# Splitting whole-array matmuls into column tiles in a four-layer recurrent kernel

## The chip, the cores and the metric

The kernel runs on one core of one Trainium2 chip. The metric is the time of one execution on the device, in microseconds; the time before is a median of three runs. The profile is that of one further execution.

## The reference

x has 32 batch rows, 128 steps and 512 features; every layer adds its result to x. In short form:

```python
x = x + einsum('bsi,io->bso', x * ys[:, None, :], W0) * d[:, None, :]      # L0, scaled by the condition
x = x + rnn(x, h0=cond)            # L1: h = tanh(h @ Wh1 + x_t @ Wx1 + b1), over 128 steps
layer = base[None] + einsum('bdr,bkr->bdk', x_a, x_b)                      # L2, rank 8, one layer per batch row
x = x + (x + einsum('btc,bco->bto', x, layer))
x = x + lstm(x, h0=cond)           # L3: four gates of 512, over 128 steps
```

`x_a` and `x_b` come from a small network on the condition (layernorm, w1, gelu, w2). The low-rank part of L2 is computed as z = x2 · x_a for each batch row, and then z · x_b.

## The kernel before

Data is feature-major: 128 partitions hold a chunk of 128 features, four chunks make 512. The 128 steps are cut into 32 tiles of 4 steps (128 tokens each). Every product in float32 precision is made of three fp16 products, high·high, high·low and low·high, accumulated in PSUM.

The four layers run as a pipeline in one loop over tiles, written out by hand as one order of work for each engine, with semaphores between them. In one turn of the loop TensorE runs, in this order:

- `lstm(t)`, `rnn(r)`, `z(a1)`, `l0(c)`, the first half of `x3_base(a1)`, `rnn(r + 1)`, `lstm(t + 1)`, `gates_x(t + 2)`, `gates_x(t + 3)`,
- `lstm(t + 2)`, `rnn(r + 2)`, the second half of `x3_base(a1)`, `x3_low_rank(a1)`, `l1(c)`, `rnn(r + 3)`, `lstm(t + 3)`, `gates_x(t + 4)`, `gates_x(t + 5)`.

The recurrent products (`rnn`, `lstm`) and `gates_x` have the state or the tokens of one step, 32 columns, as the stationary operand. They are column-tiled: four matmuls, each in its own 32 columns of the array, each with its own weight load (L1525 with 512 or 256 moving columns, L1573 with 128). The dense layers `l0`, `l1`, `x3_base` have a 128x128 block of the weight matrix as the stationary operand and the tile's 128 tokens as the moving one, in whole-array matmuls: 4 output chunks x 12 = 48 for each layer and tile, all through `split_product` (L1461). `z` and `x3_low_rank` go through it too, 24 matmuls of 64 columns each: batch rows are taken in two halves of 16, so that 16 rows x rank 8 fill the 128 partitions. Each matmul is preceded by its weight load.

VectorE masks z (`mask_z`, L1066: of all pairs of a token's and an a's batch row only the equal ones stay), and ScalarE and VectorE then split it into fp16 parts (`zm_high`, `zm_low`). VectorE's order behind `mask_z` in the loop is `zm_low`, `lstm_out`, `x1`, `rnn_sums`, `x1_low`, `rnn_out`, `lstm_gates(t + 1)`; `gates_x(t + 3)` waits for the gate sums (L1096) of the last of these. The start-up computes scales, splits all weights, and makes x_a and x_b in `w2_unit` (L1431) from w2, which streams through a ring of four buffers on SyncE's queue; each load waits for `w2_used`. `turn_a` and `move_b` bring x_a and x_b into their layout; `half_ident` and `same_b` are constants for that and for the mask. The last eight steps of the LSTM (`t >= LATE`) use matmuls of 256 columns.

Of the kernel before, what the change touches and what calls it, by code (L numbers as in the profile page):

```python
# [4 lines left out]
B, T, D, H, RANK = 32, 128, 512, 512, 8  # L5
P = 128
KC = D // P
STEPS = 4
# [6 lines left out]
BH = B // 2  # L15
ZN = STEPS * BH
RING = 4
TOP = 13
# [14 lines left out]
def build(nc, xT, condT, cond, w0, wx1, wh1, b1T, base, hw1, hb1T, hw2, hb2, ln_g, ln_b, wx3, wh3, b3, out):  # L33
# [8 lines left out]
    with ctx:  # L42
        def sb(name, shape, dt=fp32):
            return ctx.enter_context(nc.sbuf_tensor(name, shape, dt))

        def sem(name):
            return ctx.enter_context(nc.semaphore(name))
# [8 lines left out]
        base_hi, base_lo = sb("base_hi", [P, KC, D], fp16), sb("base_lo", [P, KC, D], fp16)  # L56
        a_hi, a_lo = sb("a_hi", [P, 2, KC, P], fp16), sb("a_lo", [P, 2, KC, P], fp16)
        b_hi, b_lo = sb("b_hi", [P, 2, D], fp16), sb("b_lo", [P, 2, D], fp16)
# [27 lines left out]

        half_ident = sb("half_ident", [P, 2, RH * BH])
        same_b = sb("same_b", [P, BH])

# [54 lines left out]
        kept = late[:, 1024:1024 + P]  # L144
        lstm_hs = late[:, 1024 + P:1024 + P + P // 2].bitcast(fp16)
        zm = sb("zm", [P, 2, STEPS, BH])
        zm16 = sb("zm16", [P, 2, 2, STEPS * BH], fp16)
# [61 lines left out]
        consts_ready = sem("consts_ready")  # L209
        folds_ready = sem("folds_ready")  # L210
        ys_ready = sem("ys_ready")
        dve_set = sem("dve_set")
# [53 lines left out]
        xw1_ready = sem("xw1_ready")  # L266
        z_ready = sem("z_ready")
        zm_ready = sem("zm_ready")
        base_ps, lr_ps = sem("base_ps"), sem("lr_ps")
# [22 lines left out]

        def a_turned(n, half):
            return ps_turned[n][:].rearrange("p (c b) -> p c b", b=B)[:, :, BH * half:BH * half + BH]

        def a_part(a, n, half):
            return a[:, half, 2 * n:2 * n + 2].rearrange("p k c -> p (k c)").rearrange("p (c b) -> p c b", b=BH)

# [216 lines left out]
        def _(act):  # L515
# [76 lines left out]
            def a_high():  # L592
                act.wait_ge(a_scale_ready, 1)
                for n in range(2):
                    act.wait_ge(a_ps, n + 1)
                    for half in range(2):
                        high(a_part(a_hi, n, half), a_turned(n, half), s_a).then_inc(a_hi_ready, 1)

# [213 lines left out]
        def _(dve):  # L812
# [174 lines left out]
            def a_low():  # L987
                for n in range(2):
                    dve.wait_ge(a_hi_ready, 2 * n + 2)
                    for half in range(2):  # L990
                        low(a_part(a_lo, n, half), a_turned(n, half), s_a, a_part(a_hi, n, half)).then_inc(a_lo_ready, 1)

# [71 lines left out]
            def mask_z(a):  # L1064
                dve.wait_ge(z_ready, a + 1)
                nc.vector.tensor_tensor(zm[:].rearrange("p h t b -> p (h t) b"),  # L1066
                                        ps_z[:, 0:TOK].rearrange("p (n b) -> p n b", b=BH),
                                        same_b[:].unsqueeze(1).broadcast_to([P, 2 * STEPS, BH]), ALU.mult)\
                  .then_inc(zm_ready, 1)

# [68 lines left out]
            def lstm_out(t):  # L1139
# [3 lines left out]
                if t + 1 < T:  # L1143
# [10 lines left out]
            nc.vector.tensor_reduce(fold[:], ident[:].rearrange("p (k b) -> p b k", b=B), AX.X, ALU.add).then_inc(folds_ready, 1)  # L1154
            nc.vector.tensor_reduce(same_b[:], ident[:].rearrange("p (g b) -> p b g", b=BH), AX.X, ALU.add)\
              .then_inc(folds_ready, 1)
            nc.vector.tensor_copy(half_ident[:].rearrange("p h (j b) -> p h j b", j=RH),
                                  ident[:].rearrange("p (j h b) -> p h j b", j=RH, h=2)).then_inc(folds_ready, 1)

# [238 lines left out]
        def _(pe):  # L1398
# [37 lines left out]
            def turn_a():  # L1436
                pe.wait_ge(rows_ready, 2)
                for n in range(2):
                    for k in range(2):
                        for q in range(2):  # L1440
                            at = P * (2 * k + q)
                            last = nc.tensor.transpose(ps_turned[n][:, at:at + P], a_rows[:, q, P * (2 * n + k):P * (2 * n + k) + P], ident[:])
                    last.then_inc(a_ps, 1)


            def move_b():
                pe.wait_ge(rows_ready, 5)
                pe.wait_ge(l0_scaled, LAG + 1)
                pe.wait_ge(zm_ready, 1)
                for half in range(2):  # L1450
                    for q in range(2):
                        at = BH * RH * q
                        last = nc.tensor.matmul(ps_b[half][at:at + BH * RH, :], half_ident[:, half], b_rows[:, q],
                                                start=True, stop=True, tile_position=(0, at))
                    last.then_inc(b_ps, 1)

            def split_product(psum, w_parts, x_parts):
                (w_hi, w_lo), (x_hi, x_lo) = w_parts, x_parts
                triples = [(w, x) for ws, xs_ in ((w_hi, x_hi), (w_hi, x_lo), (w_lo, x_hi)) for w, x in zip(ws, xs_)]
                for n, (w, x) in enumerate(triples):  # L1460
                    last = nc.tensor.matmul(psum, w, x, start=(n == 0), stop=(n == len(triples) - 1))  # L1461
                return last
# [5 lines left out]
            def dense(psum, w_hi, w_lo, x16, outs):  # L1468
                for oc in outs:
                    last = split_product(psum[:, TOK * oc:TOK * oc + TOK], (chunks(w_hi, oc), chunks(w_lo, oc)),  # L1470
                                         [[x16[:, part, k] for k in range(KC)] for part in range(2)])
                return last

            def of_half(x, half):
# [15 lines left out]
            def z(a):  # L1490
                pe.wait_ge(x2_lo_ready, a + 1)
                wait(pe, zm_ready, a)
                for half in range(2):
                    last = split_product(ps_z[:, ZN * half:ZN * half + ZN],
                                         [[w[:, half, k] for k in range(KC)] for w in (a_hi, a_lo)],
                                         [[of_half(x2_16[:, part, k], half) for k in range(KC)] for part in range(2)])
                last.then_inc(z_ready, 1)
# [80 lines left out]
            pe.wait_ge(consts_ready, 2)  # L1578
            pe.wait_ge(folds_ready, 3)
            pe.wait_ge(ys_ready, 2)  # L1580
# [41 lines left out]
            w2_unit(10)  # L1622
            pe.wait_ge(a_lo_ready, 4)
            z(0)
# [3 lines left out]
            w2_unit(12)  # L1628
            w2_unit(13)
            w2_unit(14)  # L1630
            pe.wait_ge(base_lo_ready, 2)
            x3_base(0, (0, 1))
            w2_unit(15)
            move_b()
            x3_base(0, (2, 3))
# [103 lines left out]
```

## Time and profile before

| | |
|---|---|
| median of three runs | 1146.4 us (1145.34 to 1146.98) |
| time of the profiled execution | 1146.9 us |
| its span, first to last instruction | 1145.1 us |
| mean granted TensorE clock | 0.995 |
| instructions | 56,238 |
| busy: TensorE matmul, weight load | 97%, 66% |
| busy: VectorE, ScalarE, GpSimd | 79%, 37%, 5% |

PE is TensorE's matmuls, PEld its weight loads, which overlap them; DVE is VectorE, ACT ScalarE, POOL GpSimd. Matmuls are pipelined, and the end of one is modelled; so the pace is read from starts. Rows name the tile written, then what is read, then shapes; "x16" counts instructions.

### The profile page before, as it was taken

To read this page: it belongs to the slowest core of one execution; us is meant where nothing else is said; L and a number is where in the kernel's file an instruction comes from. 1 tells how busy PE (TensorE), PEld (TensorE's weight loads), DVE (VectorE), ACT (ScalarE), POOL (GpSimd) and SP (SyncE) were. 2 spreads that over 40 slices of the span, in tenths; PEclk is the share of its full clock that TensorE was granted. 3 is DMA by queue.
4 is the path that set the end of the run, shared out by engine and by line. 5 is a ranking of instruction groups with operands and counts; after the bars stand their busy time and mean duration, and the time that the engine had idled before them with its cause. 6 is when DMAs were issued, how large, how long until landed. Compare 5 with 4: busy or idle time off the path is not lost.

```text
span 1145.1 us, 56238 instructions
## 1 busy us (share of the span) xinstructions
PE 1105.8 (97%) x25596; PEld 752.3 (66%) x25596; DVE 901.8 (79%) x2660; ACT 425.4 (37%) x1036; POOL 54.9 (5%) x75
## 2 busy tenths in 40 slices
PE   5779999999999999999999999999999999999997
PEld 3446666766776676667667666766776676677597
DVE  6897888878878788787778878778878877777665
ACT  6793333333333333333333333333333333333332
POOL 1000000000000000000000000000000000000000
PEclk9989999999999999999999999999999999999999
DMA  9991000000000000000000000000000000000000
GB/s 337 404 364 39 21 21 4 21 21 22 21 22 21 4 21 21 22 22 21 21 12 12 21 22 21 22 21 19 6 21 22 21 21 21 13 3 12 12 14 22
DMA packets 24606, 51.34 MB, mean 45 GB/s; under 512 B 4160, under 2 KB 4288, under 8 KB 23344
## 3 DMA queue, kind: packets, MB, share of 16 engines
q1 hardware_dynamic: 23936, 47.49, 11.7%
q8 instruction: 200, 3.28, 1.2%
q14 instruction: 38, 0.31, 0.1%
q10 hardware_dynamic: 432, 0.26, 0.1%
HBM read 39.36 MB, written 8.39 MB: 42 GB/s over the span
## 4 chain that ended last, share of the span: by engine, by line
PE 91%; DMA 3%; DVE 3%; SPq 1%; ACT 1%; issue 1%; ACTq 0%; DVEq 0%
PE ps_gates L1525 55%; PE ps_l L1461 14%; PE ps_x L1461 7%; PE ps_rnn L1573 7%; DMA ring<-in_hw 3%; PE ps_z L1461 2%; PE ps_lr L1461 2%; PE ps_l L1525 2%; SPq L398 1%; PE ps_gates L1431 1%; DMA rows<-in_ln_b 1%; SPq L429 0%; DVE gates_ring L1096 0%; ACT rows L517 0%; SPq L418 0%
## 5 line engine op out<-in xcount | busy, mean ns | idle before, releaser
L1525 PE MATMUL ps_gates<-big,lstm_h 128*32 128x512 f16 (+1 forms) x6144 | 344.1, 372 | 1.8 <-DVE lstm_h L1129 1.7
L1525 PE MATMUL ps_gates<-big,rows 128*32 128x512 f16 (+1 forms) x6144 | 343.8, 372 | 0.7 <-ACT rows L517 0.6
L1525 PEld LDWEIGHTS ps_gates<-big,rows 128*32 128x32 f16 x6144 | 167.5, 97 | 159.3 <-issue 2.6
L1525 PEld LDWEIGHTS ps_gates<-big,lstm_h 128*32 128x32 f16 x6144 | 160.9, 97 | 146.7 <-DVE lstm_h L1129 2.5
L653 ACT ACTIVATE gates_ring<-gates_ring 128x256 f32<-128x256 f32 x128 | 53.4, 417 | 303.8 <-DVE gates_ring L1096 303.8
L1096 DVE SCALAR_TENSOR_TENSOR gates_ring<-ps_gates,tile_un,rows 128x256 f32<-128x256 f32 x248 | 108.7, 478 | 49.3 <-PE ps_gates L1525 49.2
L1573 PE MATMUL ps_rnn<-wh_hi,rnn_h 128*32 128x128 f16 x4096 | 103.3, 221 | 1.6 <-ACT rnn_h L517 0.7
L1126 DVE SCALAR_TENSOR_TENSOR late<-gates_ring,tile_g,cell_tanh 128x128 f16<-128x128 f32 x127 | 44.6, 352 | 60.2 <-ACT cell_tanh L662 60.2
L1573 PEld LDWEIGHTS ps_rnn<-wh_hi,rnn_h 128*32 128x32 f16 x4096 | 71.9, 97 | 26.5 <-issue 3.8
L1461 PE MATMUL ps_l<-xs,w_hi 128*128 128x128 f16 x1024 | 79.1, 221 | 1.4 <-DVE xs L833 1.4
L1461 PE MATMUL ps_l<-x,wx_hi 128*128 128x128 f16 x1024 | 78.1, 219 | 1.6 <-DVE x L833 1.6
L1461 PE MATMUL ps_x<-x,base_hi 128*128 128x128 f16 x1024 | 78.8, 220 | 0.0
L640 ACT ACTIVATE x_ring<-rnn_pre 128x128 f32<-128x128 f32 x128 | 39.4, 308 | 71.8 <-DVE rnn_pre L924 66.1
L1461 PEld LDWEIGHTS ps_x<-x,base_hi 128*128 128x128 f16 x1024 | 61.5, 98 | 5.0 <-issue 1.8
L924 DVE SCALAR_TENSOR_TENSOR rnn_pre<-rnn_turned,un_rnn,xw1T 128x128 f32<-128x128 f32 x128 | 61.1, 477 | 4.6
L1461 PEld LDWEIGHTS ps_l<-x,wx_hi 128*128 128x128 f16 x1024 | 61.7, 98 | 3.7 <-issue 3.6
L1461 PEld LDWEIGHTS ps_l<-xs,w_hi 128*128 128x128 f16 x1024 | 62.8, 99 | 1.8 <-DVE xs L833 1.7
L517 ACT ACTIVATE rnn_h<-x_ring,scales 128x128 f16<-128x128 f32 x128 | 51.4, 402 | 4.2
L662 ACT ACTIVATE cell_tanh<-cell 128x128 f32<-128x128 f32 x128 | 39.6, 310 | 33.6 <-DVE cell L1116 33.6
L517 ACT ACTIVATE x<-x_ring,tile_s 128x512 f16<-128x512 f32 x32 | 23.1, 722 | 77.7 <-DVE x_ring L935 77.7
L1573 PE MATMUL ps_rnn<-wh_lo,rnn_h 128*32 128x128 f16 x2048 | 51.3, 220 | 0.0
L517 ACT ACTIVATE x<-x1T,tile_s 128x512 f16<-128x512 f32 x32 | 23.1, 721 | 72.6 <-DVE x1T L902 72.6
(199 smaller groups left out, 1614.2 us busy)
## 6 DMA issues: line engine op xcount, KB each, us to landing
ring<-in_hw SPq DMA_DIRECT2D x16, 1024.0 KB, 15.0
xT_sb<-in_xT SPq DMA_DIRECT2D x32, 256.0 KB, 2.8
outT<-late SPq DMA_DIRECT2D x32, 256.0 KB, 2.0
big<-in_wx SPq DMA_DIRECT2D x5, 1024.0 KB, 14.7
big<-in_wh SPq DMA_DIRECT2D x5, 1024.0 KB, 14.3
big<-in_w SPq DMA_DIRECT2D x1, 1024.0 KB, 5.9
big<-in_hw SPq DMA_DIRECT2D x1, 1024.0 KB, 13.6
late<-in_base SPq DMA_DIRECT2D x1, 1024.0 KB, 14.3
```

The costliest lines, as they stand in the source:

```text
L398: sp.dma_start(ring[:, n % RING].rearrange("p (j n) -> p j n", j=RH), hw2[q // 2, RH * (q % 2):RH * (q % 2 + 1), P * k:P * k + P].rearrang ...
L517: return nc.scalar.activation(out_, in_, ACT.Copy, scale=scale)
L640: nc.scalar.activation(x2T[i % X2_RING][:, :, s], rnn_pre[:], ACT.Tanh).then_inc(rnn_h_ready, 1)
L653: nc.scalar.activation(gates[:, 0:2 * P], gates[:, 0:2 * P], ACT.Sigmoid).then_inc(gates_acted, 1)
L662: nc.scalar.activation(cell_tanh[:], cell[:], ACT.Tanh).then_inc(cell_tanh_ready, 1)
L924: nc.vector.scalar_tensor_tensor(rnn_pre[:], rnn_turned[:], un_rnn[:], xw1T[:, :, s], ALU.mult, ALU.add).then_inc(rnn_pre_ready, 1)
L1096: nc.vector.scalar_tensor_tensor(gates[:, columns], psum[:, columns], tile_un[:, a, 0:1], b3_sb[:, columns], ALU.mult, ALU.add).then_inc(g ...
L1126: nc.vector.scalar_tensor_tensor(lstm_hs, gates[:, 2 * P:3 * P], tile_g[:, following, 1:2], cell_tanh[:], ALU.mult, ALU.mult).then_inc(lst ...
L1431: last = nc.tensor.matmul(psum[B * j:B * j + B, columns], hyperT[:, k], ring[:, n % RING, D * j + columns.start:D * j + columns.stop], sta ...
L1461: last = nc.tensor.matmul(psum, w, x, start=(n == 0), stop=(n == len(triples) - 1))
L1525: last = nc.tensor.matmul(by_chunk_of_gate(bank[B * j:B * j + B, columns]), of_step, tile_columns(w, j)[:, gates], start=start, stop=stop, ...
L1573: last = nc.tensor.matmul(by_chunk(ps_rnn[B * j:B * j + B, 0:P]), rnn_h16[:, part, k], hidden_columns(w[:, k], j), start=(n == 0 and k == ...
```

## The change

`split_product` issues each of its products as four matmuls, one for each column tile of 32 output rows; so the dense layers and the low rank have the same number of moving columns, and four times as many matmuls and weight loads. `z` no longer goes through it: x2's tokens become the stationary operand, 32 at a time (a column tile g holds the tokens whose batch row is g modulo 4), and a's columns for those 8 batch rows x 8 ranks, 64 of them, the moving one; 48 matmuls for 24. z then comes out with tokens on the partitions, so `mask_z` transposes it on VectorE in blocks of 32x32 and multiplies each half by the mask. The layout of a, the mask and the constants follow; `move_b` uses whole-array matmuls with four constant matrices (`row_picks`) and is issued in two parts.

```diff
+BG = B // KC
+BQ = BG // 2
...
-        half_ident = sb("half_ident", [P, 2, RH * BH])
-        same_b = sb("same_b", [P, BH])
+        row_picks = sb("row_picks", [P, 2, 2, P])
+        same_b = sb("same_b", [P, BQ, KC])
...
+        def by_rank(x):
+            return x.rearrange("p (k g n q j) -> p k q j n g", k=2, g=KC, n=BG, q=2)
...
                 for n in range(2):
                     act.wait_ge(a_ps, n + 1)
-                    for half in range(2):
-                        high(a_part(a_hi, n, half), a_turned(n, half), s_a).then_inc(a_hi_ready, 1)
+                    high(a_part(a_hi, n), ps_turned[n][:], s_a).then_inc(a_hi_ready, 1)
...
             def mask_z(a):
                 dve.wait_ge(z_ready, a + 1)
-                nc.vector.tensor_tensor(zm[:].rearrange("p h t b -> p (h t) b"),
-                                        ps_z[:, 0:TOK].rearrange("p (n b) -> p n b", b=BH),
-                                        same_b[:].unsqueeze(1).broadcast_to([P, 2 * STEPS, BH]), ALU.mult)\
-                  .then_inc(zm_ready, 1)
+                nc.vector.transpose(z_turned[:], by_chunk(ps_z[:, 0:2 * B])).then_inc(z_turned_ready, 1)
+                dve.wait_ge(z_turned_ready, a + 1)
+                for half in range(2):
+                    own = z_turned[:, half].rearrange("p (t b) -> p t b", t=STEPS)[:, :, BQ * half:BQ * half + BQ]
+                    last = nc.vector.tensor_tensor(zm[:, half].rearrange("p t (b g) -> p t b g", g=KC),
+                                                   own.unsqueeze(3).broadcast_to([P, STEPS, BQ, KC]),
+                                                   same_b[:].unsqueeze(1).broadcast_to([P, STEPS, BQ, KC]), ALU.mult)
+                last.then_inc(zm_ready, 1)
...
-            nc.vector.tensor_copy(half_ident[:].rearrange("p h (j b) -> p h j b", j=RH),
-                                  ident[:].rearrange("p (j h b) -> p h j b", j=RH, h=2)).then_inc(folds_ready, 1)
+            nc.vector.memset(row_picks[:], 0.0).then_inc(picks_cleared, 1)
+            dve.wait_ge(picks_cleared, 1)
+            for q in range(2):
+                for half in range(2):
+                    nc.vector.tensor_copy(row_picks[:, q, half].rearrange("p (g b q j) -> p q g b j", g=KC, b=BQ, q=2)[:, q],
+                                          ident[:].rearrange("p (j h b g) -> p h g b j", j=RH, h=2, b=BQ)[:, half])\
+                      .then_inc(folds_ready, 1)
...
-            def move_b():
-                pe.wait_ge(rows_ready, 5)
-                pe.wait_ge(l0_scaled, LAG + 1)
-                pe.wait_ge(zm_ready, 1)
+            def move_b(q):
+                if q == 0:
+                    pe.wait_ge(rows_ready, 3)
+                    pe.wait_ge(l0_scaled, LAG + 1)
+                    pe.wait_ge(zm_ready, 1)
+                else:
+                    pe.wait_ge(rows_ready, 5)
                 for half in range(2):
-                    for q in range(2):
-                        at = BH * RH * q
-                        last = nc.tensor.matmul(ps_b[half][at:at + BH * RH, :], half_ident[:, half], b_rows[:, q],
-                                                start=True, stop=True, tile_position=(0, at))
-                    last.then_inc(b_ps, 1)
+                    last = nc.tensor.matmul(ps_b[half][:], row_picks[:, q, half], b_rows[:, q], start=(q == 0), stop=(q == 1))
+                    if q == 1:
+                        last.then_inc(b_ps, 1)
...
                 for n, (w, x) in enumerate(triples):
-                    last = nc.tensor.matmul(psum, w, x, start=(n == 0), stop=(n == len(triples) - 1))
+                    for j in range(KC):
+                        last = nc.tensor.matmul(psum[B * j:B * j + B], w[:, B * j:B * j + B], x, start=(n == 0),
+                                                stop=(n == len(triples) - 1), tile_position=(0, B * j))
...
             def z(a):
                 pe.wait_ge(x2_lo_ready, a + 1)
                 wait(pe, zm_ready, a)
-                for half in range(2):
-                    last = split_product(ps_z[:, ZN * half:ZN * half + ZN],
-                                         [[w[:, half, k] for k in range(KC)] for w in (a_hi, a_lo)],
-                                         [[of_half(x2_16[:, part, k], half) for k in range(KC)] for part in range(2)])
+                for n, (part, w) in enumerate(((0, a_hi), (0, a_lo), (1, a_hi))):
+                    for k in range(KC):
+                        for g in range(KC):
+                            last = nc.tensor.matmul(ps_z[B * g:B * g + B, 0:2 * B], of_group(x2_16[:, part, k], g),
+                                                    w[:, k, 2 * B * g:2 * B * g + 2 * B], start=(n == 0 and k == 0),
+                                                    stop=(n == 2 and k == KC - 1), tile_position=(0, B * g))
                 last.then_inc(z_ready, 1)
...
             w2_unit(12)
             w2_unit(13)
+            move_b(0)
             w2_unit(14)
             pe.wait_ge(base_lo_ready, 2)
             x3_base(0, (0, 1))
             w2_unit(15)
-            move_b()
+            move_b(1)
```

## Rows read from the trace of the kernel before

**Rows 1.** The page: busy time and instructions of each engine

```profile
PE 1105.8 (97%) x25596; PEld 752.3 (66%) x25596; DVE 901.8 (79%) x2660; ACT 425.4 (37%) x1036; POOL 54.9 (5%) x75
```

**Rows 2.** The page: DMA queues (packets, MB, share of 16 engines), TensorE instructions

```profile
q8 instruction: 200, 3.28, 1.2%
```

**Rows 3.** Windows (us, busy and count by engine, PEclk, DMA): one tile

```profile
499.80:533.08 33.28, 33.28 (x772) 22.42 (x768) 26.43 (x80) 11.33 (x30) 1.73 (x2) 1.00 0.07 19
```

**Rows 4.** Timeline (start, us, what, count) of TensorE, first run and gates

```profile
503.06 0.40 PE L1573 MATMUL ps_rnn<-wh_hi,rnn_h 128*32 128x128 f16 x16
503.28 0.40 PE L1573 MATMUL ps_rnn<-wh_lo,rnn_h 128*32 128x128 f16 x16
...
503.83 0.41 PE L1461 MATMUL ps_z<-x,a_hi 128*128 128x64 f16 x8
...
504.54 0.61 PE L1461 MATMUL ps_l<-xs,w_hi 128*128 128x128 f16 x8
504.99 0.39 PE L1461 MATMUL ps_l<-xs,w_lo 128*128 128x128 f16 x4
...
509.34 2.76 PE L1525 MATMUL ps_gates<-big,lstm_h 128*32 128x512 f16 x48
511.93 1.25 PE L1525 MATMUL ps_gates<-big,rows 128*32 128x512 f16 x20
```

**Rows 5.** Timeline of TensorE, second run of the same tile

```profile
519.70 0.40 PE L1573 MATMUL ps_rnn<-wh_hi,rnn_h 128*32 128x128 f16 x16
...
521.83 0.22 PE L1461 MATMUL ps_lr<-zm,b_hi 128*128 128x64 f16 x2
...
522.52 0.61 PE L1461 MATMUL ps_l<-x,wx_hi 128*128 128x128 f16 x8
...
525.98 1.25 PE L1525 MATMUL ps_gates<-big,lstm_h 128*32 128x512 f16 x20
```

**Rows 6.** Timeline of VectorE in the same tile

```profile
507.41 0.28 DVE L1066 TENSOR_TENSOR zm<-ps_z,same_b 128x128 f32<-128x128 f32 x1
...
512.97 0.86 DVE L1096 SCALAR_TENSOR_TENSOR gates_ring<-ps_gates,tile_un,rows 128x256 f32<-128x256 f32 x2
```

**Rows 7.** Timeline of the weight loads near the end, idle before in brackets

```profile
1125.00 0.10 PEld L1525 LDWEIGHTS ps_gates<-big,rows 128*32 128x32 f16 x4 [0.42 <-issue]
...
1129.02 0.10 PEld L1525 LDWEIGHTS ps_gates<-big,rows 128*32 128x32 f16 x4 [0.54 <-issue]
...
1132.77 1.29 PEld L1525 LDWEIGHTS ps_l<-big,lstm_h 128*32 128x32 f16 x48 [0.27 <-issue]
...
1136.51 0.10 PEld L1525 LDWEIGHTS ps_gates<-big,rows 128*32 128x32 f16 x4 [0.27 <-issue]
```

**Rows 8.** Windows between such stops

```profile
1097.20:1100.67 3.47, 3.47 (x129) 3.35 (x128) 2.67 (x9) 0.46 (x2) 0.00 (x0) 1.00 0.04 9
1125.00:1129.01 4.01, 3.68 (x128) 3.48 (x128) 2.42 (x9) 0.68 (x3) 0.00 (x0) 1.00 0.02 4
1129.01:1132.75 3.74, 3.68 (x128) 3.48 (x128) 2.37 (x9) 0.62 (x3) 0.00 (x0) 1.00 0.02 4
1132.75:1136.50 3.75, 3.68 (x128) 3.48 (x128) 2.09 (x7) 1.29 (x4) 0.00 (x0) 1.00 0.02 4
```

**Rows 9.** DMA of 1126.0 to 1127.6: forty slices, and the queue

```profile
GB/s 0 0 410 0 0 0 0 0 0 0 0 0 0 0 0 0 0 0 0 0 0 0 0 0 0 0 0 0 0 0 0 0 0 0 0 0 0 0 0 0
...
q8 instruction: 1, 0.02, 5.5%
```

**Rows 10.** Timeline of TensorE in the start-up

```profile
61.30 0.23 PE L1573 MATMUL ps_rnn<-wh_hi,rnn_h 128*32 128x128 f16 x2 [0.46 <-issue]
```

**Rows 11.** Windows in the start-up, PEclk the third number from the end

```profile
79.50:82.90 3.40, 1.49 (x24) 0.41 (x16) 3.40 (x5) 2.67 (x3) 0.00 (x0) 1.00 1.04 380
82.90:86.30 3.40, 3.04 (x28) 1.77 (x29) 2.99 (x3) 2.19 (x2) 0.00 (x0) 0.50 0.33 124
```

**Rows 12.** Waits of TensorE: waiting for what, us in total, times, longest

```profile
PE ps_gates L1431 <- DMA ring<-in_hw: 11.3, 7, 4.1
```

More of the change, by code:

```diff
@@ L56, in build @@
         base_hi, base_lo = sb("base_hi", [P, KC, D], fp16), sb("base_lo", [P, KC, D], fp16)
-        a_hi, a_lo = sb("a_hi", [P, 2, KC, P], fp16), sb("a_lo", [P, 2, KC, P], fp16)
+        a_hi, a_lo = sb("a_hi", [P, KC, 2 * P], fp16), sb("a_lo", [P, KC, 2 * P], fp16)
         b_hi, b_lo = sb("b_hi", [P, 2, D], fp16), sb("b_lo", [P, 2, D], fp16)
@@ L145, in build @@
         lstm_hs = late[:, 1024 + P:1024 + P + P // 2].bitcast(fp16)
+        z_turned = sb("z_turned", [P, 2, B])
         zm = sb("zm", [P, 2, STEPS, BH])
@@ L210, in build @@
         folds_ready = sem("folds_ready")
+        picks_cleared = sem("picks_cleared")
         ys_ready = sem("ys_ready")
@@ L267, in build @@
         z_ready = sem("z_ready")
+        z_turned_ready = sem("z_turned_ready")
         zm_ready = sem("zm_ready")
@@ L291, in build, with a_part @@
         out_ready = sem("out_ready")
[L293 to L297, printed above, removed]
+        def by_rank(x):
+            return x.rearrange("p (k g n q j) -> p k q j n g", k=2, g=KC, n=BG, q=2)
+        def a_part(a, n):
+            return a[:, 2 * n:2 * n + 2].rearrange("p k c -> p (k c)")
         def by_row(w):
@@ L988, in a_low @@
                 for n in range(2):
-                    dve.wait_ge(a_hi_ready, 2 * n + 2)
-                    for half in range(2):
-                        low(a_part(a_lo, n, half), a_turned(n, half), s_a, a_part(a_hi, n, half)).then_inc(a_lo_ready, 1)
+                    dve.wait_ge(a_hi_ready, n + 1)
+                    low(a_part(a_lo, n), ps_turned[n][:], s_a, a_part(a_hi, n)).then_inc(a_lo_ready, 1)
             def base_diagonal():
@@ L1154, in _ @@
             nc.vector.tensor_reduce(fold[:], ident[:].rearrange("p (k b) -> p b k", b=B), AX.X, ALU.add).then_inc(folds_ready, 1)
-            nc.vector.tensor_reduce(same_b[:], ident[:].rearrange("p (g b) -> p b g", b=BH), AX.X, ALU.add)\
+            nc.vector.tensor_reduce(same_b[:], ident[:].rearrange("p (g b r) -> p b g r", g=KC, b=BQ), AX.X, ALU.add)\
               .then_inc(folds_ready, 1)
-            nc.vector.tensor_copy(half_ident[:].rearrange("p h (j b) -> p h j b", j=RH),
-                                  ident[:].rearrange("p (j h b) -> p h j b", j=RH, h=2)).then_inc(folds_ready, 1)
+            nc.vector.memset(row_picks[:], 0.0).then_inc(picks_cleared, 1)
[5 more added lines that the diff above has]
+                      .then_inc(folds_ready, 1)
             dve.wait_ge(ld_cond, 16)
@@ L1440, in turn_a @@
                         for q in range(2):
-                            at = P * (2 * k + q)
-                            last = nc.tensor.transpose(ps_turned[n][:, at:at + P], a_rows[:, q, P * (2 * n + k):P * (2 * n + k) + P], ident[:])
+                            last = nc.tensor.transpose(by_rank(ps_turned[n][:])[:, k, q],
+                                                       a_rows[:, q, P * (2 * n + k):P * (2 * n + k) + P], ident[:])
                     last.then_inc(a_ps, 1)
-            def move_b():
-                pe.wait_ge(rows_ready, 5)
-                pe.wait_ge(l0_scaled, LAG + 1)
-                pe.wait_ge(zm_ready, 1)
-                for half in range(2):
-                    for q in range(2):
-                        at = BH * RH * q
-                        last = nc.tensor.matmul(ps_b[half][at:at + BH * RH, :], half_ident[:, half], b_rows[:, q],
-                                                start=True, stop=True, tile_position=(0, at))
-                    last.then_inc(b_ps, 1)
+            def move_b(q):
[5 more added lines that the diff above has]
+                    pe.wait_ge(rows_ready, 5)
+                for half in range(2):
+                    last = nc.tensor.matmul(ps_b[half][:], row_picks[:, q, half], b_rows[:, q], start=(q == 0), stop=(q == 1))
+                    if q == 1:
+                        last.then_inc(b_ps, 1)
             def split_product(psum, w_parts, x_parts):
@@ L1472, in dense, with of_group @@
                 return last
+            def of_group(x, g):
+                return x.rearrange("p (n g) -> p g n", g=KC)[:, g]
             def of_half(x, half):
@@ L1492, in z @@
                 wait(pe, zm_ready, a)
-                for half in range(2):
-                    last = split_product(ps_z[:, ZN * half:ZN * half + ZN],
-                                         [[w[:, half, k] for k in range(KC)] for w in (a_hi, a_lo)],
-                                         [[of_half(x2_16[:, part, k], half) for k in range(KC)] for part in range(2)])
+                for n, (part, w) in enumerate(((0, a_hi), (0, a_lo), (1, a_hi))):
[4 more added lines that the diff above has]
+                                                    stop=(n == 2 and k == KC - 1), tile_position=(0, B * g))
                 last.then_inc(z_ready, 1)
@@ L1578, in _ @@
             pe.wait_ge(consts_ready, 2)
-            pe.wait_ge(folds_ready, 3)
+            pe.wait_ge(folds_ready, 6)
             pe.wait_ge(ys_ready, 2)
@@ L1622, in _ @@
             w2_unit(10)
-            pe.wait_ge(a_lo_ready, 4)
+            pe.wait_ge(a_lo_ready, 2)
             z(0)
```

## The prediction

> **What bounds the kernel now.** I read the page first, then the windows of one tile, then the order of time on TensorE, and last the issue gaps near the end. The page shows TensorE busy for 97% of the span [rows 1]. In the middle of the loop that is no average over good and bad stages: the window of one tile, 33.28 us, is busy for all of it, at a granted clock of 1.00 [rows 3]. So in the loop every us that TensorE gains or loses is a us of the result, unless something else ends last.
>
> The order of time gives the paces. Column-tile matmuls of 128 columns (rnn) come in fours, one per tile: sixteen take 503.28 - 503.06 = 0.22 us, so a four takes 55 ns [rows 4]. A whole-array matmul of 128 columns takes 0.45/8 = 56 ns. So the split costs no array time by itself. The 48 of rnn would be through at 503.06 + 3 x 0.22 = 503.72, yet the first z matmul starts at 503.83: changing between column tiles and the whole array costs about 0.10 us [rows 4]. A tile changes four times, so 0.41 us go there. z takes 0.71 us (24 matmuls of 64 columns, 29.6 ns each) [rows 4], the low rank 0.69 us for as many [rows 5].
>
> The view that decides is another one. TensorE runs 25,596 matmuls and as many weight loads [rows 1], and the instruction queue brought 200 packets of 16.4 KB [rows 2]: 3.28 MB over 51,192 instructions is 64 bytes each, so one packet is a page of 256 instructions, 128 pairs. Near the end TensorE's weight loads stop again and again "on issue", with no semaphore named: at 1125.00, 1129.02, 1132.77 and 1136.51 [rows 7]. Between one of these stops and the next lie exactly 128 weight loads and 128 matmuls [rows 8]: the stops are page turns. The same kind of gap stands in the start-up, at 61.30 us [rows 10].
>
> What a turn costs: from one starved turn to the next took 4.01, 3.74 and 3.75 us; one more page, from 1097.20 on, took 3.47 us, all of it filled with work [rows 8]. After the turn at 1125.00 the next page's packet starts in the third of forty slices of its window, about 1.1 us later, and moves for 5.5% of 16 x 1.6 us = 1.4 us [rows 9]; the next turn at 1129.02 comes 1.5 us after that. So a page is asked for when the one before it is entered, one at a time, and is there 1.1 + 1.4 + 1.5 = 4.0 us later. Over the run a packet took 1.2% x 16 x 1145.1 / 200 = 1.1 us [rows 2], so 3.7 us is the usual case. **I take 3.7 us per page, with 3.5 and 4.0 as bounds.** In the loop this hides today, barely: the stretch from rnn to rnn around z and l0 holds 384 instructions in 509.34 - 503.06 = 6.28 us [rows 4], 4.2 us per page, and its twin around the low rank as many in 6.28 us [rows 5].
>
> The Trainium skill says otherwise: "Runtime: NRT & Kernel Launch", section "Instruction fetch mechanics", gives TensorE an instruction buffer of 128 KiB (2,048 instructions), refilled in 16 KiB blocks, the crossing mostly hidden. The block size agrees with the trace; the depth does not, since a turn waits for the very next page here. By that rule the fetch would cost nothing (first rival).
>
> **The change part by part, for one tile of the loop.**
>
> Dense layers and low rank: 3 x 48 + 24 = 168 whole-array matmuls become 672; z's 24 become 48. A tile goes from 768 pairs (772 with those in flight at the edges of the window) [rows 3] to 768 + 504 + 24 = 1,296 pairs, 2,592 instructions, 10.1 pages for 6.0.
>
> Array time: z in twelve fours of 64 columns. The trace shows no such four; its cost lies between 29.6 ns (one z matmul) and 55 ns (an rnn four). I take the first, since the fours of 128 columns stream at the pace of one matmul: 12 x 29.6 = 0.36 us, 0.36 less (0.05 at the other bound). The low rank's fours lie between the same bounds: nothing, to +0.62 us. The dense layers: nothing. Four changes of mode gone: -0.41. Together 0.77 us less, **if instructions arrive**.
>
> They do not. The gates' matmuls of 512 columns take 511.93 - 509.34 = 2.59 us per 96 instructions [rows 4], 6.9 us a page, and hide any fetch. Between them lie two runs. Run 1 (rnn, z, l0, half of x3_base, rnn) becomes 96 + 96 + 384 + 192 + 96 = 864 instructions; at the array's own pace 6.28 - 0.20 - 0.36 = 5.72 us, 6.6 ns each, 1.70 us a page. Run 2 (rnn, half of x3_base, low rank, l1, rnn) becomes 96 + 192 + 192 + 384 + 96 = 960; 6.28 - 0.20 = 6.08 us, 1.62 us a page. A run starts and ends somewhere inside a page: on average the first half page was asked for in the gates and is there, the last half runs at its own pace, and the F/256 - 1 pages between cost 3.7 us each.
> - Run 1: 2.375 x 3.7 + 1.70 = 10.5 us for 6.28.
> - Run 2: 2.75 x 3.7 + 1.62 = 11.8 us for 6.28.
> - The page that a run ends in was asked for at its last turn; where more than about 157 of its 256 instructions belong to the run, the gates wait for the next one too: in 4 of 10 cases, 1 us on average, twice: +0.7.
>
> Sum: 4.2 + 5.5 + 0.7 = **+10.4 us per tile, 29 tiles: +302 us**. At 3.5 us a page it is 5.1 x 0.2 = 1.0 less per tile, at 4.0 us 1.5 more: +272 to +345.
>
> mask_z: one VectorE instruction of 0.28 us [rows 6] becomes a transpose and two half-size products behind a wait. No row shows these; each has half the elements, so between 0.14 and 0.28 us, 0.42 to 0.84 together. I take 0.62, +0.34. Behind it on VectorE stand zm_low, x1, rnn_sums and the gate sums, which end at 512.97 + 0.86 = 513.83 [rows 6]; TensorE needs them about 514.3 (half-way through the two gates_x, one four ahead). Today 0.34 us would nearly fill that room; with TensorE 4 us later in run 1 it is covered. If that cover is gone, see the first rival.
>
> Start-up: l0, l1 (three each), one x3_base, one low rank and one z add 7 x 288 + 144 + 48 = 2,208 instructions, 8.6 pages at 2.0 us more than their own pace: +17. TensorE waits 11.3 us there for w2's transfers [rows 12], which cover part. I take +8, with 0 and +25 as bounds. move_b's first half (two whole-array products for two split ones) goes into such a wait, its second half costs what the whole did. row_picks, a_high and a_low are set-up in waits: nothing, at most +1.
>
> End: two more rounds of z, x3_base and low rank add 960 instructions, 3.75 pages, in a stage already at the page's pace, partly under waits for lstm_h: +6 (2 to 12).
>
> Clock: where TensorE was busy 1.49 of 3.40 us, the granted clock of the next 3.4 us was 0.50, the lower level [rows 11]. The new runs are busy 1.7 of 3.7 us, about that. Inside a run the lower clock costs little (32 fours at twice 55 ns are 3.5 us, under 3.7), but gates behind it would run at half pace until the clock is back: at most 1.7 us per run, 3.4 per tile. I take 0.5 per tile, +15; bounds 0 and +99.
>
> Sum against the profiled execution (span 1145.1, its time 1146.9, 0.5 over the median): 1146.9 + 302 + 8 + 6 + 15 = **1478 us**.
>
> **The rivals.**
> 1. *The fetch stays hidden*: TensorE holds several pages ahead, and a turn never waits. Then 0.77 us per tile are free, but run 1's 0.56 meet VectorE: its chain to the gate sums does not shrink and grows by 0.34, against some 0.42 us of room, so that stretch keeps about 0.1; run 2 keeps 0.2. 29 x 0.3 = 9, and 2 at the ends: 1136 us; 1123 if VectorE kept up. It decides from the point where a page turn costs less than 1.7 us. Against it: three pages in a row of 3.7 to 4.0 us, each ended by a gap [rows 7, 8]. 5%. The page of the Trainium skill named above would give this case.
> 2. *A starved sequencer asks earlier*, so that transfer and landing alone count, 1.1 + 1.5 = 2.6 us: runs of 7.9 and 8.8 us, +4.1 per tile, 1146.9 + 119 + 8 = 1274 us. Against it: the packet of [rows 9] started 1.1 us after the turn, though TensorE was starving. 6%.
> 3. *The clock falls behind each run*: 1478 + 29 x 2.9 = 1562 us. For it stands [rows 11]; against it, that runs at the lower clock are busy enough to bring it back. 12%.
> 4. *No change within 0.2%*: a page of about 2.0 us would do it; nothing points there. 1%.
>
> **How the numbers follow.** The forecast has 76%. Its own range is 1440 to 1540 (page 3.5 to 4.0 us, the start-up's bounds). To leave out no more than 2 in 10, I reach up into rival 3 and a little below for pages that overlap with gates better than on average: 1395 to 1580. A measurement of this kernel tells 0.2% from no change; faster 5%, same 1%, slower 94%.
>
> **What the profile afterwards would show.** TensorE's busy share falls to about 80%, with gaps "on issue" inside l0, l1, x3_base and the low rank, 128 pairs apart; the instruction queue brings some 330 packets; a tile takes about 44 us; no gap at the old changes of mode; z fours 29.6 ns apart; VectorE's share falls. I am wrong if 128 pairs of l1 pass in 1.8 us, or if the gaps name a semaphore; too low if the granted clock falls well under 0.9.

## The result, and the profile after

The changed kernel takes 1454.7 us (median of six runs, 1450.64 to 1469.17) for 1145.05 (six runs): a ratio of 1.272, 95% interval 1.266 to 1.278. It is slower by 310 us. 1478 was forecast, with a range of 1395 to 1580. The profiled execution is the slowest of the six, 1469.2 us, so the rows below hold some 14 us more than the median.

The page after, against [rows 1, 2]: TensorE's busy share, the granted clock in forty slices, the instruction queue.

```profile
PE 1165.1 (79%) x42492; PEld 853.1 (58%) x42492; DVE 902.8 (62%) x2726; ACT 426.8 (29%) x1034; POOL 54.4 (4%) x75
...
PEclk9789999999999999989999999989999999999999
...
q8 instruction: 332, 5.44, 1.5%
```

TensorE is busy for 79% (forecast: about 80%), and the queue brought 332 packets (forecast: some 330) for 200. Its busy time grew by 59 us only; 263 us of the 322 by which the span grew are time in which it does nothing. The two spans, cut at the first matmul of `rnn(8)`, in the loop's first turn, and of `rnn(124)`, 29 turns later; windows as in [rows 3], of the changed kernel:

```profile
0.00:125.86 125.86, 82.87 (x2271) 50.48 (x2273) 83.10 (x216) 74.00 (x102) 6.28 (x19) 0.86 0.72 261
125.86:1384.18 1258.32, 1011.49 (x37591) 743.79 (x37587) 769.19 (x2343) 331.05 (x869) 48.10 (x56) 0.97 0.05 16
1384.18:1467.37 83.19, 70.73 (x2645) 58.85 (x2637) 50.53 (x167) 21.78 (x63) 0.00 (x0) 0.98 0.04 14
```

and of the kernel before:

```profile
0.00:102.92 102.92, 71.63 (x1164) 44.26 (x1168) 82.56 (x212) 74.17 (x104) 6.66 (x19) 0.95 0.87 318
102.92:1068.80 965.88, 965.48 (x22276) 649.94 (x22272) 769.47 (x2285) 329.57 (x869) 48.23 (x56) 1.00 0.06 18
1068.80:1145.14 76.34, 68.67 (x2164) 58.08 (x2156) 49.76 (x163) 21.68 (x63) 0.00 (x0) 1.00 0.04 14
```

The start-up took 22.9 us more, the loop 292.4 (10.1 per tile), the end 6.9. What TensorE waited for inside the loop (waits: us, times, longest us):

```profile
PE ps_l L1475 <- issue: 137.7, 85, 2.6
PE ps_x L1475 <- issue: 37.1, 22, 2.1
PE ps_lr L1475 <- issue: 29.5, 20, 1.9
PE ps_rnn L1593 <- issue: 28.4, 19, 2.0
PE ps_gates L1545 <- issue: 13.0, 14, 2.0
```

246 us, and all of it "issue": no semaphore, no engine and no transfer of data is named. The only row beside these is a single wait of 0.7 us for VectorE. The timeline of the second run of one tile (starts and, in brackets, idle time before), to be held against [rows 5]:

```profile
666.96 0.40 PE L1593 MATMUL ps_rnn<-wh_hi,rnn_h 128*32 128x128 f16 x16
...
667.62 0.63 PE L1475 MATMUL ps_x<-x,base_hi 128*32 128x128 f16 x32
...
670.95 0.21 PE L1475 MATMUL ps_lr<-zm,b_hi 128*32 128x64 f16 x4 [1.60 <-issue]
...
672.22 0.35 PE L1475 MATMUL ps_l<-x,wx_hi 128*32 128x128 f16 x11
674.80 0.49 PE L1475 MATMUL ps_l<-x,wx_hi 128*32 128x128 f16 x21 [2.23 <-issue]
...
677.31 0.54 PE L1475 MATMUL ps_l<-x,wx_lo 128*32 128x128 f16 x11
678.54 0.37 PE L1475 MATMUL ps_l<-x,wx_lo 128*32 128x128 f16 x5 [0.69 <-issue]
...
679.41 2.79 PE L1545 MATMUL ps_gates<-big,lstm_h 128*32 128x512 f16 x48
```

The run takes 679.41 - 666.96 = 12.45 us for 6.28. It stops three times, in the middle of the low rank and twice in the middle of l1's products, where nothing is being waited for. The windows between the stops count the instructions:

```profile
670.94:674.79 3.85, 1.63 (x127) 1.46 (x128) 2.24 (x6) 1.41 (x2) 0.00 (x0) 1.00 0.02 4
674.79:678.53 3.74, 3.06 (x128) 2.85 (x128) 0.18 (x1) 0.00 (x0) 0.00 (x0) 0.59 0.02 4
```

The DMA's view of the 2 us behind the first stop shows what is on its way (forty slices, and the queue):

```profile
GB/s 0 0 0 0 0 0 0 0 0 0 0 0 0 0 0 0 0 0 0 0 0 0 328 0 0 0 0 0 0 0 0 0 0 0 0 0 0 0 0 0
...
q8 instruction: 1, 0.02, 4.2%
```

Again 128 weight loads and 128 matmuls, a page, in 3.85 and 3.74 us, of which TensorE worked for 1.63 in the first. The next page's packet starts in the 23rd of forty slices, 671.0 + 22 x 0.05 = 672.1, 1.15 us after the turn at 670.95. It moves for 4.2% of 16 x 2 us = 1.34 us, to 673.5, and the next turn comes 1.3 us later: the three parts of [rows 9] again. These two pages are no exception: in the trace of the loop one such stop follows another with just one page between them 95 times, and from stop to stop it takes 3.74 us on average, 3.45 to 4.12.

In the second window the granted clock is 0.59, after a page in which the array had been busy for 1.63 of 3.85 us. Where it falls late in a run, the gates behind the run pay, as behind the first run of this tile (timeline of TensorE, and the window of the first twelve fours):

```profile
654.85 4.52 PE L1545 MATMUL ps_gates<-big,lstm_h 128*32 128x512 f16 x48
659.18 5.36 PE L1545 MATMUL ps_gates<-big,rows 128*32 128x512 f16 x96
664.37 2.77 PE L1545 MATMUL ps_gates<-big,lstm_h 128*32 128x512 f16 x48
```

```profile
654.85:659.18 4.33, 4.33 (x59) 1.95 (x52) 1.69 (x4) 0.71 (x2) 0.00 (x0) 0.59 0.02 4
```

Twelve fours take 659.18 - 654.85 = 4.3 us there, busy throughout, at a granted clock of 0.59; the twelve that start at 664.37 are through at 666.96, 2.6 us later, as in [rows 4].

### The profile page after: what moved, and what is told of

It reads as the page before. It is cut to its first block, busy times and chain, and to the rows that moved or that the text cites. A ratio compares the mean times of both kernels' runs of the same rounds, so it can differ in the third digit from the quotient of the medians.

```text
span 1467.4 us, 90094 instructions
## 1 busy us (share of the span) xinstructions
PE 1165.1 (79%) x42492; PEld 853.1 (58%) x42492; DVE 902.8 (62%) x2726; ACT 426.8 (29%) x1034; POOL 54.4 (4%) x75
## 4 chain that ended last, share of the span: by engine, by line
PE 78%; issue 19%; DVE 2%; ACT 1%; DMA 1%; ACTq 0%; DVEq 0%
PE ps_gates L1545 45%; PE ps_l L1475 14%; PE ps_rnn L1593 6%; PE ps_x L1475 6%; PE ps_lr L1475 2%; PE ps_l L1545 1%; PE ps_z L1514 1%; PE ps_gates L1443 1%; DMA rows<-in_ln_b 1%; DVE big L837 0%; DVE gates_ring L1103 0%; PE ps_lr L1443 0%; ACT big L522 0%; PE ps_l L1466 0%; PE ps_gates L1438 0%
## 5 line engine op out<-in xcount | busy, mean ns | idle before, releaser
L1545 PE MATMUL ps_gates<-big,lstm_h 128*32 128x512 f16 (+1 forms) x6144 | 366.5, 381 | 14.9 <-issue 13.4
L1475 PE MATMUL ps_l<-x,wx_hi 128*32 128x128 f16 x4096 | 96.4, 230 | 65.2 <-issue 65.2
L1475 PE MATMUL ps_l<-xs,w_hi 128*32 128x128 f16 x4096 | 90.3, 224 | 44.7 <-issue 42.7
L1475 PEld LDWEIGHTS ps_l<-x,wx_hi 128*32 128x32 f16 x4096 | 73.4, 102 | 70.4 <-issue 70.4
L1475 PE MATMUL ps_x<-x,base_hi 128*32 128x128 f16 x4096 | 88.2, 222 | 23.0 <-issue 23.0
L1475 PEld LDWEIGHTS ps_l<-xs,w_hi 128*32 128x32 f16 x4096 | 68.9, 99 | 50.1 <-issue 47.7
L1475 PEld LDWEIGHTS ps_x<-x,base_hi 128*32 128x32 f16 x4096 | 70.5, 98 | 26.0 <-issue 25.9
L1475 PE MATMUL ps_l<-x,wx_lo 128*32 128x128 f16 x2048 | 62.2, 232 | 25.6 <-issue 25.6
L1475 PE MATMUL ps_l<-xs,w_lo 128*32 128x128 f16 x2048 | 58.2, 224 | 20.7 <-issue 20.7
L1475 PE MATMUL ps_x<-x,base_lo 128*32 128x128 f16 x2048 | 59.7, 223 | 16.3 <-issue 16.1
L1475 PEld LDWEIGHTS ps_l<-x,wx_lo 128*32 128x32 f16 x2048 | 43.5, 104 | 30.3 <-issue 30.3
```

Of the source, the lines that this page charges most:

```text
L1475: last = nc.tensor.matmul(psum[B * j:B * j + B], w[:, B * j:B * j + B], x, start=(n == 0), stop=(n == len(triples) - 1), tile_position=(0, ...
L1545: last = nc.tensor.matmul(by_chunk_of_gate(bank[B * j:B * j + B, columns]), of_step, tile_columns(w, j)[:, gates], start=start, stop=stop, ...
```

## The experiments

The times of before on the same chip were 1144.8 us (the first four) and 1145.4 (the others).

**1. Column tiles for z alone.** `split_product` is whole-array again; everything else is as changed.

```diff
-                    for j in range(KC):
-                        last = nc.tensor.matmul(psum[B * j:B * j + B], w[:, B * j:B * j + B], x, start=(n == 0),
-                                                stop=(n == len(triples) - 1), tile_position=(0, B * j))
+                    last = nc.tensor.matmul(psum, w, x, start=(n == 0), stop=(n == len(triples) - 1))
```

> The changed kernel with the dense layers and the low rank whole-array again: only z's column tiles, its mask and layout are new. A tile has 792 pairs for 768. Page theory (a page of 128 pairs takes 3.7 us from being asked for to being there, and only short runs of TensorE that cross pages pay): 1,584 instructions per tile, the runs stay near 3.4 us a page, nothing is starved; TensorE saves up to 0.36 us per tile and VectorE's longer mask takes some of it back: 1141 us, 1134 to 1150. Rival, every added column-tile pair costs the same (the 310 us over 29 tiles and 528 pairs are 20 ns each): 24 pairs, +0.5 us per tile, 1160 us. Rival, the longer mask delays the gates: +0.3 us per tile, 1155 us.

1141.35 us, ratio 0.9969 (0.9956 to 0.9981): 0.3% faster, and where the page theory put it. z's part of the change isn't what costs; all that was lost belongs to the split. z in the timeline of TensorE:

```profile
501.00 0.30 PE L1512 MATMUL ps_z<-a_hi,x 128*32 128x64 f16 x16
...
501.26 0.33 PE L1512 MATMUL ps_z<-a_hi,x 128*32 128x64 f16 x16
501.52 0.62 PE L1474 MATMUL ps_l<-xs,w_hi 128*128 128x128 f16 x8
```

The mask in the timeline of VectorE:

```profile
504.69 0.24 DVE L1069 STREAM_TRANSPOSE z_turned<-ps_z 128x64 f32<-128x64 f32 x1
504.96 0.36 DVE L1073 TENSOR_TENSOR zm<-z_turned,same_b 128x64 f32<-128x64 f32 x2
505.70 0.29 DVE L837 SCALAR_TENSOR_TENSOR zm<-zm 128x128 f16<-128x128 f32 x1 [0.38 <-ACT zm L522]
```

z and the change of mode behind it take 501.52 - 501.00 = 0.52 us; with 0.10 for the change of mode, z's twelve fours take 0.42 (forecast 0.36, bounds 0.36 and 0.66). The mask takes 505.32 - 504.69 = 0.63 us (forecast 0.62). From `rnn(8)` to `rnn(124)` a tile takes 33.15 us for 33.31 before, less than the first run alone gained.

**2. The split alone.** The kernel before, with the change's `split_product`.

```diff
-                    last = nc.tensor.matmul(psum, w, x, start=(n == 0), stop=(n == len(triples) - 1))
+                    for j in range(KC):
+                        last = nc.tensor.matmul(psum[B * j:B * j + B], w[:, B * j:B * j + B], x, start=(n == 0),
+                                                stop=(n == len(triples) - 1), tile_position=(0, B * j))
```

> The kernel before with only the split of the dense layers and the low rank; z stays whole-array. Page theory: 2,544 instructions per tile for 2,592, the two runs have 816 and 960: a tile of 43.2 us at 3.7 us a page, 1446 us, 1425 to 1465. Rival, z's new form and its mask are what costs: about 1146 us. Equal cost of each added pair does not differ here (504 of 528 pairs: 1440 us).

1495.0 us, ratio 1.306, above the stated range: the expectation had counted wrongly. In the kernel before z goes through `split_product` too, so the edit makes 96 column-tile pairs of z's 24, where the expectation left z alone. The page (TensorE, instruction queue):

```profile
PE 1170.1 (78%) x44028; PEld 858.0 (58%) x44028; DVE 891.1 (60%) x2660; ACT 426.9 (29%) x1036; POOL 54.2 (4%) x75
...
q8 instruction: 344, 5.64, 1.6%
```

44,028 matmuls, 1,536 more than the change's 42,492, which is 48 for each of 32 tiles. 96 instructions more in the first run are 96 / 256 x 3.7 = 1.39 us a tile, 40 us over 29 tiles; the kernel takes 1495.0 - 1454.7 = 40.3 us more than the change. The number on record was a miss, and the agreement afterwards is in part luck: between the two traces a tile grows by 0.83 us only (44.22 for 43.39; 24 us over 29 tiles), the first run by 1.07 (11.40 for 10.33) where 1.39 are worked out. That the first run pays for the added instructions is shown, the price of 3.7 us only roughly.

**3. Two column tiles of 64 rows** for four of 32, in all that the change splits.

```diff
-                    for j in range(KC):
-                        last = nc.tensor.matmul(psum[B * j:B * j + B], w[:, B * j:B * j + B], x, start=(n == 0),
-                                                stop=(n == len(triples) - 1), tile_position=(0, B * j))
+                    for j in range(2):
+                        last = nc.tensor.matmul(psum[2 * B * j:2 * B * j + 2 * B], w[:, 2 * B * j:2 * B * j + 2 * B], x, start=(n == 0),
+                                                stop=(n == len(triples) - 1), tile_position=(0, 2 * B * j))
```

> The changed kernel with the split in two column tiles of 64 output rows for four of 32: 960 pairs per tile for 1,296 (768 before). Page theory: the two runs have 576 instructions each, 2.2 pages, of which some 1.2 turns lie inside and about half are hidden by the gates beside them; replayed at 3.7 us a page a tile takes 34.1 us: +0.85 us over 29 tiles and about 8 at the start, 1178 us, 1160 to 1195. Rival, each added pair costs 20 ns: 192 pairs, +3.8 us per tile, 1256 us. Rival, column tiling of these products costs whatever the number of tiles: over 1400 us.

1165.0 us, ratio 1.0175 (1.016 to 1.019). The cost is not so much per pair: 192 of the 528 added pairs per tile, 36%, bring 20 of the 310 us, 7%. A tile takes 33.88 us (forecast 34.1), and the start-up loses nothing (`rnn(8)` at 102.8 us), where 8 was expected. The timeline shows one thing more:

```profile
493.62 0.40 PE L1593 MATMUL ps_rnn<-wh_hi,rnn_h 128*32 128x128 f16 x16
493.95 0.64 PE L1475 MATMUL ps_x<-x,base_hi 128*64 128x128 f16 x16
```

The last sixteen of rnn would be through at 493.62 + 0.22 = 493.84; the first product in tiles of 64 rows starts 0.11 us later. Going from tiles of 32 to tiles of 64 costs what going to the whole array costs [rows 4]. The Trainium skill's "TensorEngine Tiling (Array Packing)", section "Key Properties", says that changing the tiling mode drains the engine; this agrees.

**4. The same tiles in fewer instructions.** The dense layers with tokens as the stationary operand. Those layers' results have tokens where the reference has features.

```diff
-                for oc in outs:
-                    last = split_product(psum[:, TOK * oc:TOK * oc + TOK], (chunks(w_hi, oc), chunks(w_lo, oc)),
-                                         [[x16[:, part, k] for k in range(KC)] for part in range(2)])
+                columns = slice(P * outs[0], P * outs[-1] + P)
+                pairs = [(part, w, k) for part, w in ((0, w_hi), (1, w_hi), (0, w_lo)) for k in range(KC)]
+                for n, (part, w, k) in enumerate(pairs):
+                    for j in range(KC):
+                        last = nc.tensor.matmul(psum[B * j:B * j + B, columns], x16[:, part, k, B * j:B * j + B], w[:, k, columns],
+                                                start=(n == 0), stop=(n == len(pairs) - 1), tile_position=(0, B * j))
```

> The changed kernel with the three dense layers turned round: the tokens are the stationary operand, 32 to a column tile, the weights the moving one, 512 columns (256 in the halves of the base layer). Column tiles, products and array time are those of the change (12 fours of 216 ns for 48 of 56 ns), in a quarter of the instructions (half for the base layer): 912 pairs per tile. The dense layers' results come out with tokens on the partitions, which the rest takes as if they were features. Page theory: runs of 480 and 576 instructions, a tile of 33.4 us at 3.7 us a page, 1150 us, 1135 to 1165. Rival, column tiling of these products is what costs: like the change, 1455 us. Rival, 20 ns for each added pair: 144 pairs, 1230 us.

1157.2 us, ratio 1.0107 (1.009 to 1.012). Against the change, the column tiles and the number of products are the same and the array time nearly so, and all but 12 of its 310 us are gone with 768 of the 2,592 instructions of a tile. A first run in which no page was late, in the timeline of TensorE:

```profile
505.73 0.44 PE L1596 MATMUL ps_rnn<-wh_hi,rnn_h 128*32 128x128 f16 x16
...
506.89 1.91 PE L1488 MATMUL ps_l<-w_hi,xs 128*32 128x512 f16 x32
...
509.48 1.06 PE L1488 MATMUL ps_x<-base_hi,x 128*32 128x256 f16 x32
...
511.46 0.83 PE L1548 MATMUL ps_gates<-big,lstm_h 128*32 128x512 f16 x12
```

511.46 - 505.73 = 5.73 us, the array's own pace that the prediction had worked out for this run (5.72). The column tiles do what was promised of them. What is left of the loss is mostly the same wait: 13.4 us on "issue" in the loop, where a tile takes 33.53 us for 33.15 in experiment 1.

**5. Half the array work in as many instructions.** `parts` is 2 for the dense layers, 1 for the low rank.

```diff
+                each, size = len(triples) // parts, x_hi[0].shape[-1] // parts
...
+                    own = slice(size * (n // each), size * (n // each) + size) if parts > 1 else slice(None)
...
-                        last = nc.tensor.matmul(psum[B * j:B * j + B], w[:, B * j:B * j + B], x, start=(n == 0),
-                                                stop=(n == len(triples) - 1), tile_position=(0, B * j))
+                        last = nc.tensor.matmul(psum[B * j:B * j + B, own], w[:, B * j:B * j + B], x[:, own],
+                                                start=(n % each == 0), stop=(n % each == each - 1), tile_position=(0, B * j))
```

> The changed kernel with half the array work in the dense layers: of the twelve products of a chunk six go over the first 64 tokens and six over the other 64, so half of each layer's products are left out. The number of instructions is that of the change. By the array's own pace a tile would lose 144 fours x 27 ns = 3.8 us. Page theory: the inner pages of a run take 3.7 us whatever they hold, and the replay at 3.7 us a page gives 43.48 us per tile for 43.53: 1452 us, 1430 to 1470 (the array is busy still less, so the lower clock may come more often). Rival, the array or the tiled matmuls themselves set the time of the change: 29 x 3.8 less, 1345 us.

1537.8 us, 83 us more than the change, with half of the dense work left out. Windows of two pages in one second run (low rank, l1, rnn):

```profile
649.27:652.84 3.57, 1.30 (x128) 1.17 (x127) 2.16 (x6) 1.41 (x2) 0.00 (x0) 0.76 0.02 5
652.84:656.31 3.47, 2.11 (x128) 1.84 (x128) 0.31 (x1) 0.00 (x0) 0.00 (x0) 0.50 0.02 5
```

The page, the granted clock in forty slices:

```profile
PEclk9688888887887888787888887877888877878999
```

The gates behind that run, in the timeline of TensorE:

```profile
657.16 4.88 PE L1547 MATMUL ps_gates<-big,lstm_h 128*32 128x512 f16 x48
661.82 5.40 PE L1547 MATMUL ps_gates<-big,rows 128*32 128x512 f16 x96
```

A page still takes 3.57 and 3.47 us, so a run is as long as with the full work: over 29 tiles, between the starts of the matmuls that bound them, 10.56 and 11.72 us for the change's 10.33 and 11.49. The rival that the array sets the time is out. Why it is slower is the clock: the expectation had named it as possible and left no room for its price. In those two pages TensorE was busy for 1.30 and 2.11 us, at a granted clock of 0.76 and 0.50, and the twelve fours behind them took 4.7 us (657.16 to 661.82) for 2.6. In the loop 381 fours of the gates ran at half pace, about 0.21 us late each: 80 us. In the change's trace there are 49, 10 us.

**6. Only l1 split**, on top of experiment 1; the added argument is the number of column tiles, 1 elsewhere.

```diff
-                last = dense(ps_l1, wx1_hi, wx1_lo, x1_16, outs)
+                last = dense(ps_l1, wx1_hi, wx1_lo, x1_16, outs, KC)
```

> The kernel with column tiles for z alone, and of the dense layers only l1 in four column tiles: 936 pairs per tile. Page theory: run 2 (rnn, half of the base layer, low rank, l1, rnn) goes from 384 to 672 instructions, 2.6 pages, the first run stays as it is; the replay gives +2.16 us per tile at 3.7 us a page, 29 tiles and about 6 at the start: 1141 + 69 = 1210 us, 1190 to 1225. Rival, 20 ns for each added pair wherever it stands: 144 pairs and 32 tiles, 1233 us. Rival, the dense layers' split is free as long as one layer alone is split: 1141 us.

1200.0 us, ratio 1.047 (1.045 to 1.049), within the range and 33 us under what the cost per pair gives. A tile takes 34.78 us, 1.63 more than in experiment 1 (forecast 2.16), and nearly all of it in the second run, 7.68 us for 6.28 between the starts that bound it. Why it is 0.5 us less than the expectation's replay of the page rule gave wasn't separated.

**7 and 8. VectorE's chain.** `zm_low` behind `lstm_out` in the loop, with z alone in column tiles and in the kernel before.

```diff
-                zm_low(a1)
                 lstm_out(t)
+                zm_low(a1)
```

> Column tiles for z alone, with VectorE's zm_low behind lstm_out in the loop. In the run with z alone VectorE stood idle for 0.38 us ahead of zm_low, waiting for ScalarE's high part, so the move shortens its chain to the gate sums by about that. If the longer mask is what kept TensorE at 33.11 us per tile where its best tiles took 33.00, the waits for the gate sums go and all tiles take 33.00: 27 x 0.11 = 3 us less, 1138 us, 1136.5 to 1140. If pages are what the worse tiles wait for: no change, 1141.

> The kernel before with the same move of zm_low. There TensorE was busy for the whole of a tile and waited for no gate sums, so a shorter chain on VectorE is worth nothing: 1145 us, within 0.2%. If it gains as much as with z in column tiles, the gain of the run before this one does not belong to z.

With z in column tiles 1137.7 us, ratio 0.9931 (0.9919 to 0.9943); in the kernel before 1144.7, 0.9995 (0.9986 to 1.0004). Between experiments 1 and 7 lie 3.6 us (4.2 when each is held against the kernel before on its own chip), for the 3 expected; between their traces a tile loses 0.11 us, 3.1 over 29 tiles. Waits of the weight loads in the loop (us, times, longest), experiment 1:

```profile
PEld ps_gates L1543 <- DVE gates_ring L1103: 10.6, 27, 0.7
```

and experiment 7:

```profile
PEld ps_gates L1543 <- DVE gates_ring L1103: 2.1, 9, 0.6
```

27 waits for the gate sums became nine, and the tile 33.04 us for 33.15. This is the fastest version found: z in column tiles, the dense layers and the low rank whole-array, `zm_low` later.

## Why the prediction was right

The mechanism was right in every part that decides: one page of 128 pairs ahead, asked for at the turn, about 3.7 us a page. Only sizes were off, and some of them cancelled: the loop was forecast 25 us too long (302 + 15 for 292), the start-up 15 us too short. That the sum lies only 9 us from the profiled execution is in part luck.

- **The two runs.** +4.2 and +5.5 us were forecast; between the starts of the matmuls that bound them they take 10.33 and 11.49 us on average over 29 tiles, 6.29 before: +4.04 and +5.20. The page was priced well (3.74 us from stop to stop), so a run pays for about a tenth of a page less than was counted. Experiments 2 and 6 fell short in the same direction; why wasn't separated.
- **The gates behind them.** Forecast +0.7 us per tile for late pages and +0.5 for the clock. The two stages of gates take 10.78 us each for 10.37: +0.82 per tile. 49 fours at half pace are 10 us of the 24 over the loop (15 forecast); the wait row of the gates has the other 13 (20 forecast). The bound of 1.7 us per run for the clock held here, but it isn't general: behind one run of experiment 5 twelve fours lost 4.66 - 2.59 = 2.07 us.
- **The loop together**: 4.04 + 5.20 + 0.82 = 10.1 us per tile, 292 us. Forecast: 302 + 15.
- **Start-up**: the mis-sized term, +22.9 us for +8, inside its bounds of 0 and 25. The 11.3 us of waits for w2 [rows 12] were used up as cover; no such row is left. Behind it stand late pages, one of them later than any in the loop, in a stretch in which the DMA engines were busy throughout with the start-up's loads, and a lower clock, 0.86 on average for 0.95. By the windows above, 11.2 us of the 22.9 are busy time of TensorE (82.87 for 71.63) and 11.7 idle time; how much of the busy time is the clock's wasn't separated. The waits on "issue" in the start-up, the late page's row in the timeline of TensorE, and the window around it (the last numbers: clock, DMA share, GB/s):

```profile
PE ps_l L1475 <- issue: 16.6, 7, 4.5
PE ps_lr L1475 <- issue: 2.4, 1, 2.4
```

```profile
70.09 0.93 PE L1475 MATMUL ps_l<-x,wx_hi 128*32 128x128 f16 x25 [4.50 <-issue]
```

```profile
52.00:74.00 22.00, 14.54 (x438) 9.59 (x430) 14.16 (x29) 14.23 (x19) 1.13 (x2) 0.81 1.00 388
```

- **End**: +6.9 for +6.
- **Array time**: z's fours 0.42 us for the 0.36 taken; no 0.10 us at the old changes of mode. Run at the array's pace, as in experiment 4, the first run needs the 5.73 us worked out. So the saving exists, and the pages hide it.
- **mask_z**: 0.63 us for 0.62. With TensorE late it costs nothing: the wait rows of the changed loop name no gate sums. With TensorE in time it does: experiments 1 and 7 show the room at the gate sums used up, as the first rival had it.
- **The rivals.** Hidden fetch: out, by the stops and by experiments 3 to 5. An earlier request: out, the packet started 1.15 us after the turn. The clock behind each run: not in the change (49 fours in 29 tiles), but it is what experiment 5 shows once the runs are less busy: 1538 us, in another kernel, so that it lies near the 1562 worked out for this rival says little. No change: by the prediction's own terms the two runs would have stayed at 6.28 us with a page of 1.8 us, (2 x 6.28 - 1.70 - 1.62) / 5.125, not of 2.0. By the Trainium skill's "Runtime: NRT & Kernel Launch", section "Instruction fetch mechanics", the first rival would have come true, since a crossing is called mostly hidden; the rows of the changed kernel's loop, with waits of up to 2.6 us, don't bear that out.

The sum was 1478 against a profiled execution of 1469.2. Why six runs of one kernel spread over 1.3%, where the kernel before spreads over 0.24%, wasn't tried.

## What to carry to other kernels

Count instructions as well as columns: four matmuls in four column tiles cost the array what one costs, but they are four times the instructions, and in a stretch with under 3.7 us of work per 256 instructions it is the pages that set the pace. A split pays where it lowers the columns (z here). Between long matmuls, which hide the pages, it should cost less; no run tries that apart. One operand turned round so that fewer and longer matmuls fill the same tiles took nearly all of the loss away. A gap "on issue" every 128 pairs is the sign; the packets of the instruction queue give the size of a page, and with it the number of pages of a changed kernel in advance.

## What the runs showed of the hardware that was not expected

- Less work in a starved stretch made the kernel slower: halving the dense layers' columns left the pages at the same pace (3.57 and 3.47 us in the run shown) and put 381 fours of 512 columns, for 49, at half pace behind it (1537.8 us for 1454.7).
- Changing from column tiles of 32 rows to tiles of 64 costs the 0.1 us that changing to the whole array costs.
